# Sorted experts with a stationary first layer, and a last sublayer that adds its tiles into the output

## What is computed

```python
# layer 2, feed-forward: after its own attention, one expert per token
logits = hn2 @ gate_w + gate_b
idx = jnp.argmax(logits, axis=-1)
mid = jax.nn.relu(jnp.einsum('th,ehf->etf', hn2, w1) + b1[:, None, :])
y = jnp.einsum('etf,efh->eth', mid, w2) + b2[:, None, :]
moe = y[idx, jnp.arange(hn2.shape[0])]
return x + moe.reshape(b, s, h)

# layer 3, feed-forward: the last sublayer, two experts per token
score = jax.nn.relu(xf @ rw1 + rb1) @ rw2 + rb2
_, topi = jax.lax.top_k(score, TOP_K)
mask = jnp.zeros(score.shape, bool).at[jnp.arange(T)[:, None], topi].set(True)
gate = jax.nn.softmax(jnp.where(mask, score, -jnp.inf), axis=-1)
for e in range(N_EXPERTS):
    h = jax.nn.relu(xf @ W1[e] + b1[e])
    y = h @ W2[e] + b2[e]
    out = out + gate[:, e:e + 1] * y
```

## Time and profile before

| what | value |
|---|---|
| median of 3 runs | 3084.59 us (3083.26 to 3086.73) |
| the profiled execution's own time | 3088.82 us |
| its span | 3087.1 us |
| PE, PEld busy | 2636.8 us (85%), 1818.8 us (59%) |
| DVE, ACT, POOL busy | 1844.1 us (60%), 1224.8 us (40%), 767.0 us (25%) |

### The profile page before, as it was taken

How to read it: one execution, slowest core, us unless ns; L and a number is a source line. 1 busy time by engine, 2 the same in 40 slices (tenths; PEclk the granted TensorE clock), 3 DMA queues, 4 the chain that set the end, 5 groups by cost and what they waited for, 6 DMA issues and landing times. The chain is left out here.

```text
span 3087.1 us, 45580 instructions
## 1 busy us (share of the span) xinstructions
PE 2636.8 (85%) x15125; PEld 1818.8 (59%) x15125; DVE 1844.1 (60%) x4065; ACT 1224.8 (40%) x3138; POOL 767.0 (25%) x589
## 2 busy tenths in 40 slices
PE   3998989999688885999989989779869687969996
PEld 1565756666455454767767767546635566446664
DVE  6885886589788544343455579743355678343333
ACT  2223654266687134433434446412122566312221
POOL 4433430054000322222212246311110233121110
PEclk8999999999887797999999999879979888989998
DMA  9001000000200433000010020321110300431113
GB/s 308 1 1 47 13 19 1 15 1 1 62 4 1 112 88 135 1 1 1 1 38 16 6 69 2 119 94 32 48 49 1 87 11 1 162 103 32 33 33 101
DMA packets 155926, 142.87 MB, mean 46 GB/s; under 512 B 59012, under 2 KB 141972, under 8 KB 155316
## 3 DMA queue, kind: packets, MB, share of 16 engines
q1 hardware_dynamic: 139684, 109.58, 12.3%
q0 software_dynamic: 8688, 23.82, 2.2%
q10 hardware_dynamic: 7328, 6.56, 0.7%
HBM read 97.12 MB, written 42.81 MB: 45 GB/s over the span
## 5 line engine op out<-in xcount | busy, mean ns | idle before, releaser
L958 POOL TENSOR_TENSOR room<-room 128x1024 f32<-128x1024 f32 x144 | 273.3, 1898 | 466.6 <-DVE room L893 465.9
L887 DVE TENSOR_REDUCE room<-room 128x8 f32<-128x1024 f32 x144 | 174.0, 1208 | 0.0
L1400 PE MATMUL l3f_hidden<-room,Y 128*128 x312 | 146.2, 612 | 1.2 <-DVE Y L1644 1.2
L1419 PE MATMUL l3f_out<-room,Y 128*128 x624 | 141.1, 379 | 1.4 <-DVE Y L1669 1.4
L1419 PEld LDWEIGHTS l3f_out<-room,Y 128*128 128x128 f32 x624 | 118.5, 190 | 33.9 <-issue 19.8
L958 POOL TENSOR_TENSOR room<-room,Y 128x1024 f32<-128x1024 f32 x32 | 60.7, 1898 | 252.0 <-DVE Y L893 252.0
L1777 POOL DMA_INDIRECT results<-Y,l3f_dest x39 | 37.5, 962 | 295.7 <-DVE Y L1677 288.2
L614 PE MATMUL l2a_proj<-room 128*128 128x256 f32 x384 | 97.7, 399 | 11.6 <-ACT room L982 11.6
L1030 ACT ACTIVATE room<-l2a_scores,Y 128x128 f32<-128x128 f32 x256 | 72.1, 381 | 86.6 <-DVE Y L879 86.6
L1749 ACT ACTIVATE Y<-l3f_hiddenT,vecs 128x128 f32<-128x128 f32 x156 | 44.6, 368 | 155.1 <-PE l3f_hiddenT L1410 155.1
L2379 POOL DMA_INDIRECT sorted_rows<-room,l1f_place_i x32 | 31.1, 970 | 262.7 <-DVE l1f_place_i L2090 253.5
(11 more groups left out here) (827 smaller groups left out, 6842.4 us busy)
## 6 DMA issues: line engine op xcount, KB each, us to landing
sorted_rows<-head SPq DMA_DIRECT2D x1, 16512.0 KB, 66.6
room<-in_L_ffn_w SPq DMA_DIRECT2D x16, 1024.0 KB, 12.4
room<-in_L_ffn_W SPq DMA_DIRECT2D x16, 1024.0 KB, 12.5
Y<-sorted_rows SPq DMA_DIRECT2D x62, 129.0 KB, 2.1
room<-in_ctx SPq DMA_DIRECT2D x24, 256.0 KB, 2.8
room<-results SPq DMA_DIRECT2D x12, 512.0 KB, 7.2
room<-sorted_rows SPq DMA_DIRECT2D x39, 129.0 KB, 2.1
Y<-results SPq DMA_DIRECT2D x8, 512.0 KB, 7.9
```

What stands on the lines that cost most here:

```text
L887: dve.tensor_reduce(rsum[:, u % 2, :], p[:, u % (TURN + 1), :, :], AX.X, ALU.add)
L958: pool.tensor_tensor(p[:, u % (TURN + 1), :, :], p[:, u % (TURN + 1), :, :], rinv[:, u % (TURN + 1), :].unsqueeze(2).to_broadcast([P, HEAD ...
L1400: mm = pe.matmul(hbank[a][:, :], rowsT[:, n % 2, kc, :], chip.room[:, bass.ds(at + (kc * F + a * half_f), half_f)], start=(kc == 0), stop= ...
L1419: mm = pe.matmul(obank[n % 2][:, 0:D], hT[:, f, :], chip.room[:, bass.ds(at + (SLOT // 2 + f * D), D)], start=(f == 0), stop=(f == HC - 1))
```

## The change

Names first. `stage` is a new view of two times 128x2048 elements in `yn`, the buffer of the normalised rows, which nobody needs once the scatters have landed. `so_far` is a 128x256 piece of `chip.Y`. `ROW` goes from 258 to 260.

1. *First layer.* ACT copies the tile's first-layer weights to `stage` (`stage_weights`), two tiles ahead. PE uses pieces of 128x128 of them as the stationary operand and streams the 128 turned rows, so the hidden units come out with the units on the partitions. `turn_hidden` and both `empty_hidden` are gone, and `relu` reads the first layer's banks; these are now four, two for even and two for odd tiles. `hT` has two buffers. PE turns tile n+2 after first layer n+1.
2. *Last sublayer.* SP stores x to the output at the block's start. For each tile POOL fetches the output rows that the tile belongs to, DVE multiplies the result with its gate and adds the fetched rows, and POOL scatters the sum back; fetch n waits for scatter n-1. Rows beyond the tile's real ones fall out of bounds and are not moved. The gates are computed per routing group, go through the table beside the token's number, and no results are loaded back at the end.
3. *Routing with a flat router (l2fm).* The order on PE and DVE is changed: normalisation runs two groups ahead and logits one ahead, and the additions `X += Y` stand at other places.
4. *End of l2fm.* Token numbers are laid out so that a partition's results lie in consecutive rows. Half of each group's statistics are made by ACT (means and squares by accumulation), half by DVE. The next block's loads are issued by SP behind the gathers and not by ACT.
5. *l1x.* ACT clears v in two passes in place of POOL; the square roots come first on ACT, and DVE takes their reciprocals later.

```diff
-                def first_layer(n, at):
+                def first_layer(n):
                     pe.wait_ge(rowsT_ready, n + 1)
+                    pe.wait_ge(staged, n + 1)
                     for a in range(2):
-                        if n:
-                            pe.wait_ge(h_copied[a], n)
-                        for kc in range(KC):
-                            mm = pe.matmul(hbank[a][:, :], rowsT[:, n % 2, kc, :], chip.room[:, bass.ds(at + (kc * F + a * half_f), half_f)],
-                                           start=(kc == 0), stop=(kc == KC - 1))
+                        if n >= 2:
+                            pe.wait_ge(hT_ready[a], n - 1)
+                        for q in range(HS):
+                            f = a * HS + q
+                            for kc in range(KC):
+                                mm = pe.matmul(hidden[n % 2][a][:, q * P:(q + 1) * P], stage[:, n % 2, kc * F + f * P:kc * F + (f + 1) * P], rowsT[:, n % 2, kc, :],
+                                               start=(kc == 0), stop=(kc == KC - 1))
                         mm.then_inc(h_filled[a], 1)
...
+                def stage_weights(n):
+                    at = act.value_load(weights_at[0:1, n:n + 1], min_val=0, max_val=(NE - 1) * SLOT)
+                    act.copy(stage[:, n % 2, :], chip.room[:, bass.ds(at, KC * F)]).then_inc(staged, 1)
+
+                act.wait_ge(w.v["landed"], 32 * NE)
+                act.wait_ge(scattered, 16 * NB * keep)
+                for n in range(2):
+                    stage_weights(n)
                 for n in range(NT):
                     relu(n)
-                    if n + 1 < NT:
-                        empty_hidden(n + 1)
-                if prefetch:
+                    if n + 2 < NT:
+                        stage_weights(n + 2)
+                if not last:
                     act.preload_act_table(ACT.Sqrt)
-                    act.wait_ge(out_filled, NT)
-                    prefetch.load(act)
+                    for g in range(NG):
+                        act.wait_ge(combined, g + 1)
+                        for b in range(g * GR + 2, (g + 1) * GR):
+                            act.activation(back[0][:, b, :], chip.X[:, b, :], ACT.Identity, scale=1.0 / D, accum_out=chip.mv[:, b, 0:1])
+                        act.drain()
+                        for b in range(g * GR + 2, (g + 1) * GR):
+                            op = act.activation(back[0][:, b, :], chip.X[:, b, :], ACT.Square, bias=chip.mv[:, b, 0:1], scale=-1.0, accum_out=chip.mv[:, b, 1:2])
...
+                if last:
+                    pool.wait_ge(x_stored, 16 * NG)
                 for n in range(NT):
                     pool.wait_ge(dest_ready, n + 1)
+                    if last:
+                        if n:
+                            pool.wait_ge(out_ready, n)
+                            pool.wait_ge(returned[(n - 1) % 2], ((n - 1) // 2 + 1) * 16)
+                        pool.indirect_dma_start(so_far, None, final_rows, bass.IndirectOffsetOnAxis(dest[:, n % 2:n % 2 + 1], 0),
+                                                bounds_check=TOK - 1, oob_is_err=False).then_inc(fetched, 16)
                     pool.wait_ge(out_ready, n + 1)
...
-                    dve.tensor_tensor(result[:, n % 2, :], obank[n % 2][:, 0:D], w.v["b2"][:, bass.ds(at, D)], ALU.add).then_inc(out_ready, 1)
+                    op = dve.tensor_tensor(result[:, n % 2, :], obank[n % 2][:, 0:D], w.v["b2"][:, bass.ds(at, D)], ALU.add)
+                    if last:
+                        op.then_inc(out_emptied, 1)
+                        dve.drain()
+                        dve.wait_ge(fetched, 16 * (n + 1))
+                        op = dve.scalar_tensor_tensor(out=result[:, n % 2, :], in0=result[:, n % 2, :], scalar=gate[:, n % 2, 0:1], in1=so_far,
+                                                      op0=ALU.mult, op1=ALU.add)
+                    op.then_inc(out_ready, 1)
...
-                    for k in range(NG + 1):
-                        if first_turned <= k < NG:
-                            turn_rows(k)
-                        if k < NG:
-                            logits_flat(k)
-                        if k:
-                            rank(k - 1)
-                        if k < NG:
-                            logits_back(k)
+                    if not first_turned:
+                        turn_rows(0)
+                    logits_flat(0)
+                    for k in range(NG):
+                        if k == 0:
+                            turn_rows(1)
+                        logits_back(k)
+                        if k + 1 < NG:
+                            logits_flat(k + 1)
+                        rank(k)
+                        if k + 2 < NG:
+                            turn_rows(k + 2)
...
             @block.gpsimd
-            def _(pool):
-                pool.memset(v[:, :, :, :], 0.0).then_inc(v_zeroed, 1)
```

210 lines of the change are left out of this document (135 added, 75 removed).

## The result

The changed kernel takes 3006.12 us (median of 4 runs, 3004.09 to 3009.43) where the kernel before took 3083.93 on the same chip: a ratio of 0.9756, 95% interval 0.9741 to 0.9770. The forecast was 2987 with a range of 2972 to 3013. The profiled execution spans 3004.2 us, 82.9 less than before.

What follows compares the result with a forecast made beforehand. It took TensorE to set the pace of both tile loops, with TensorE idle in the other stretches changed. Savings 34 + 26 + 21 - 0.8 + 8 + 7 + 2.5 = 97.7 us from 3084.6 gave 2987, range 2972 to 3013.

Steps and rivals of the forecast that it cites:

- First layer stationary: Tiles of l3f and l2fm: short matmuls 0.111 us apart make a tile 7.36 us, saving 34 and 26 us.
- The tile of 10.6 us: Counter-case from the Trainium skill: weight loads not overlapped, about 214 ns per instruction, so a tile slower than now.
- rival 4: Tiles of both loops: short matmuls space at 0.13 us or more, 40 us less saved, 3027; chance 3%.
- The chain on GpSimd: l3f, per tile: hop, scatter, hop, fetch, add in series take 7.36 us (6.4 at best), equal to TensorE's tile.
- Rival 1: l3f: the serial fetch and scatter order becomes the bound at 7.6 to 8.5 us a tile; 3012; chance 18%.
- l3f's end: From VectorE's last tile to the span's end: 5.3 us instead of 26.6, saving 21 us, bounds 19 to 22.
- Routing and l2fm's end: l2fm: reordered routing saves 8 us (bounds 4 to 10), its end 7 us (bounds 3 to 10).
- Rival 2: Tile loops gain as forecast, but routing, l2fm's end and l1x give nothing: 17.5 us less, 3004; chance 10%.
- The router's term: l3f's routing: computing gates before the places go to GpSimd adds 0.8 us once to the path.
- l1x: Start of l1x: zeroing moved to ScalarE and earlier roots save 2.5 us; bounds 5.5 saved to 4 lost.
- Rival 3: l3f: under a busy memory the serial transfers take 13.2 us a tile, slower than before, 3215; chance 4%.

Runs made afterwards that it cites:

- e1: Changed kernel with the last sublayer's old end back (results table, gathers, combining and stores at the end, no adding into the output); ratio 0.9731.
- e9: Changed kernel with an accumulating scatter in memory replacing fetch, add and scatter, a table copy at the end, and four place and gate buffers; ratio 0.9701.
- e3: Changed kernel without fetch, add and scatter of the last of the 39 tiles, which holds no token; ratio 0.9752.
- e11: Changed kernel with a GpSimd drain added behind every fourth tile's fetch in the last sublayer; ratio 0.9763.
- e6: Changed kernel with l2fm's routing put back in the old order; ratio 0.9799.
- e7: Changed kernel with l2fm's old end: old results layout, gau's weights issued by ScalarE before the gathers, all statistics on VectorE; ratio 0.9800.
- e10: Changed kernel with the last sublayer's old end back, and results laid out so its gathers read 4 KB runs; ratio 0.9729.
- e8: Changed kernel with l1x's old start: GpSimd zeroes, VectorE adds epsilon beside it, ScalarE takes roots behind its selector copies; ratio 0.9762.
- e5: The changed kernel itself run once more, unaltered, beside other experiments on another chip; ratio 0.9769 to the kernel before.

## Why the prediction was right, and where 19 us were lost

**First layer stationary: right.** The spacing is 0.11 us as worked out from the turns, and the tile is 7.24 us and not 7.36: the 0.11 that I added for the change of shape is not there. Hence 29.0 in l2fm for 26. With the chain gone l3f runs at 7.24 too (e1, e9). The tile of 10.6 us that I had set against this part and rival 4 (spacing of 0.13) are out. ScalarE's copy of 128x2048 takes 1.91 us and nobody waits for it.

**The chain on GpSimd: the step "that equals TensorE's 7.36, so the chain just hides or just shows" failed on the side that I thought less likely.** Its size was well estimated: 7.36 us against 7.46 in the regular turn, the fetch 2.81 for 2.96. But I compared it with a tile that is 0.12 too long, and with no spread: of 66 transfers 9 to 13 are 0.6 to 2.2 us late, which costs 0.4 to 0.5 us a tile. A chain without slack takes all of that on; e9, with slack, does not feel it. Together l3f's tiles lost 37 x 0.59 = 21.8 us of what they could have gained (e1), of which the forecast's longer tile hid four, so that the term was 16.5 for 34. Rival 1 is what came, with 7.83 a tile for its 7.6 to 8.5, though not quite as it said: the parts of a turn sum to 7.46, and 12.6 of the 21.8 us are late transfers, which it did not have.

**l3f's end: the term "bias 0.42, gate-and-add 0.42 with a drain, scatter, end" left out two things.** The last fetch stands behind the scatter ahead and its landing (2988.39 to 2991.95, 3.6 us), and "end" is GpSimd's drain of 10.27 us (e3, e11). So 15.8 us for 5.3, and a saving of 10.7 for 21. The drain stood in the profile of before with 7.05 us, begun at 3061.5 just behind the last scatter; I did not ask what an end without its gathers would uncover.

**Routing and l2fm's end: right.** 7.3 and 7.3 us by the two profiles; undone they cost 8.9 (e6) and 8.8 (e7), which is nearer to the better bound of 10 in both. The parts of the end came as worked out: landing 2.4 for 2.4, gather 2.5 for 1.8, sums and statistics 2.0 for 2.5. Rival 2 is out. **The router's term had the wrong sign:** 0.8 us lost in the sum, 1.0 gained in the profiles. The price of the gates on the way does not show: up to the first tile e1 and e10, without them, take 109.7 and 110.3 us, the other profiles with the change 109.8 to 110.9. Where the gain over the 111.0 of before comes from, no run shows.

**l1x: mis-sized low, and not sure.** 6.2 in the two profiles for 2.5, of it 2 to 3 the clock (3.2 to 4.2 between profiles that are alike, e8). The ScalarE passes that I feared cost no more than 1.2 us as far as e8 shows, not nothing and not the several us of my worst bound.

**Rival 3** (a chain of over 9.9 us under a busy memory) did not come: behind tile 1 no turn of the chain in the profile after was over 9.7 us (9.9 in e3 and e5 to e8), and the usual fetch and scatter were 2.8 and 2.5.

In sum the sublayers that the change touches gave 78.0 us for 97.7; the missing 20 are 17.5 of l3f's tiles and 10.3 of its end, less 8 that l2fm, l1x and the router gave beyond the forecast. Another 4.9 came from sublayers that the change leaves alone, and the median moved by 77.8. So part of it is luck: the range held because it was drawn wide enough for most of rival 1, and because some 8 us of terms that were set too low and 5 us from elsewhere made up for half of what the two failed steps lost. Without the 5 us the time would be 3011, 2 us inside the range.
